# Routing of a part spread over seven half-pairs of units, its column sums beside the router products, and the scatters of the first two parts later

## What is computed

```
x = x + xattn(layernorm(x), ctx_1024, Wq, Wk, Wv, Wp, bp, ln_g, ln_b)
x = x + ffn(layernorm(x), W_gate_router, expert_bias, Wg, Wu, Wd, Wg_s, Wu_s, Wd_s)

# xattn: 16 heads of 16; q and k are layer-normed per head, q scaled by 0.5
attn = softmax(einsum(q, k)); out = (attn @ v) @ Wp.T + bp

# ffn, for each row x of 4096: 8 experts of width 192, the two best are taken
scores = sigmoid(x @ W_gate_router)
_, sel = top_k(scores + expert_bias, 2)
w      = scores[sel] / (scores[sel].sum() + 1e-20)
out    = silu(x @ Wg_s) * (x @ Wu_s) @ Wd_s                    # shared expert
out   += sum over the two of w * (silu(x @ Wg[e]) * (x @ Wu[e])) @ Wd[e]
```

## The kernel before

| unit | 15 | 16 | 17 | 18 | 19 |
|---|---|---|---|---|---|
| part 0 before | scored, best(0) | taken(0), best(1) | taken(1), counted | sums_of, weights | places_of |

## Time and profile before

### The profile page before, as it was taken

The page is one execution under the profiler, slowest core; times in us unless marked ns, Lnnn a source line. Parts: engine busy times, 40 slices in busy tenths (PEclk is TensorE's granted clock), DMA queues, the critical chain, the costliest instruction groups (busy, mean ns, idle before and its releaser), DMA issues.

```text
span 578.1 us, 11042 instructions
## 1 busy us (share of the span) xinstructions
PE 495.2 (86%) x2876; PEld 286.7 (50%) x2877; DVE 344.2 (60%) x1028; ACT 241.4 (42%) x470; POOL 232.4 (40%) x206
## 2 busy tenths in 40 slices
PE   4827879999978988988898993599999999999990
PEld 3724324444434443333554551376676676676660
DVE  5776447767788768645779622155555555555550
ACT  0255767788867776766421110122222222222210
POOL 5354222111111473045114545046646546655534
PEclk9956989999999999989999999699999999999996
DMA  8911911111111221033325574245655656756634
GB/s 274 358 71 27 367 45 43 51 38 38 37 38 37 75 93 56 19 111 128 113 97 175 177 227 173 74 74 83 108 102 83 117 84 93 118 92 86 118 44 46
DMA packets 43766, 60.58 MB, mean 105 GB/s; under 512 B 6512, under 2 KB 34800, under 8 KB 43120
## 3 DMA queue, kind: packets, MB, share of 16 engines
q1 hardware_dynamic: 28688, 36.92, 20.8%
q0 software_dynamic: 15040, 23.21, 20.7%
HBM read 33.77 MB, written 29.52 MB: 109 GB/s over the span
## 4 chain that ended last, share of the span: by engine, by line
PE 52%; DVE 16%; DMA 10%; issue 8%; ACT 8%; POOL 4%; POOLq 1%; SPq 1%; DVEq 0%; ACTq 0%
PE bankS L1050 15%; PE bankS L1066 9%; PE bankV L896 5%; DMA sorted_rows<-XR,route 4%; DMA out<-VR,attn 4%; PE bankR L771 3%; PE bankQ L771 3%; POOL sorted_rows L495 3%; ACT attn L642 3%; PE bankV L900 2%; PE bankS L883 1%; PE bankD L1039 1%; PE bankQ L1057 1%; PE bankV L1039 1%; PE bankR L1057 1%
## 5 line engine op out<-in xcount | busy, mean ns | idle before, releaser
L550 POOL DMA_INDIRECT out<-VR,attn x72 | 111.2, 1544 | 101.0 <-DVE VR L1466 53.4
L1050 PE MATMUL bankS<-experts,scores_in 128*128 x288 | 104.7, 496 | 1.5 <-issue 0.6
L495 POOL DMA_INDIRECT sorted_rows<-XR,route x64 | 63.3, 989 | 96.9 <-DVE XR L1338 23.3
L642 ACT ACTIVATE attn<-bankS,bias 128x512 f32<-128x512 f32 x128 | 81.0, 681 | 11.2 <-PE bankS L871 11.1
L1066 PE MATMUL bankS<-experts,scores_in 96*128 x288 | 74.3, 380 | 1.1 <-DVE scores_in L1457 1.1
L747 ACT ACTIVATE scores_in<-bankS 128x192 f32<-128x192 f32 x72 | 23.8, 330 | 109.6 <-PE bankS L1050 102.4
L1050 PEld LDWEIGHTS bankS<-experts,scores_in 128*128 128x128 f32 x288 | 52.3, 192 | 33.6 <-issue 10.5
L896 PE MATMUL bankV<-attn,VS 128*32 128x512 f32 x256 | 63.5, 619 | 5.3 <-DVE OTT L1245 4.0
L898 PE MATMUL bankD<-attn,ON 128*32 128x512 f32 x256 | 63.5, 619 | 0.0
L1451 DVE TENSOR_TENSOR scores_in<-scores_in,bankS 128x192 f32<-128x192 f32 x72 | 25.5, 354 | 51.4 <-ACT scores_in L747 40.0
L435 POOL DMA_DIRECT2D x_in<-in_xT x13 | 9.5, 734 | 113.7 <-PE bankQ L771 112.7
(11 more groups left out here) (253 smaller groups left out, 864.7 us busy)
## 6 DMA issues: line engine op xcount, KB each, us to landing
VS<-sorted_rows SPq DMA_DIRECT2D x72, 130.0 KB
x_cols<-X2T SPq DMA_DIRECT2D x16, 256.0 KB, 2.2
out<-X SPq DMA_DIRECT2D x8, 512.0 KB
x_in<-in_xT POOLq DMA_DIRECT2D x15, 256.0 KB, 3.2
scores_in<-x_cols SPq DMA_DIRECT2D x14, 256.0 KB
experts<-in_wgu SPq DMA_DIRECT2D x2, 1536.0 KB, 9.5
X<-in_x SPq DMA_DIRECT2D x1, 2048.0 KB, 16.7
experts<-in_wd SPq DMA_DIRECT2D x2, 768.0 KB, 16.8
```

The costliest lines, as they stand in the source:

```text
L495: pool.indirect_dma_start(sorted_rows.rearrange("s p r -> (s p) r"), bass.IndirectOffsetOnAxis(ap=index, axis=0), rows, None, bounds_check ...
L550: pool.indirect_dma_start(out, bass.IndirectOffsetOnAxis(ap=dest[:, i:i + 1], axis=0), y_out[:, i % 4], None, bounds_check=B * N + SPARE - ...
L642: act.activation(Pb[:, u % 2, c, :], bankS[:, c % GH, :], ACT.Exp, bias=bias[:, b, GH * g + c:GH * g + c + 1] if c < GH else biasR[:, b, g ...
L1050: last = pe.matmul(gate_bank(k)[:, 0:2 * F], x_col[:, k, c * P:(c + 1) * P], rhs, start=(c == 0), stop=(c == KC - 1))
```

## The change

In the loop, the routing of parts 0 and 1 is laid out anew; the steps and their order are the same.

| unit | 15 | 16 | 17 | 18 | 19 | 20 | 23 |
|---|---|---|---|---|---|---|---|
| part 0 now | scored | best(0) | taken(0) | best(1) | taken(1), counted | sums_of, weights | places_of |

Part 1 follows eight units later: scored in unit 23 (behind places_of of part 0), up to places_of in unit 31. Part 2 begins with scored in unit 31, and its best(0) moves into the tail. TensorE's `counts` moves from the unit with piece 6 (10) to the unit with piece 7 (11), ahead of the router products in the same bank; its results go to the last 16 columns of bankR, which those products don't touch, and the wait for `r_based` moves on with it. Part 0's scatters wait for `pv_ready` 22 up to 29. Part 1's scatters are not edited, but their places are now ready in unit 31 and no longer in unit 27.

```
-                        pool.wait_ge(pv_ready, UNITS // 2 + 2 + j // 2)
+                        pool.wait_ge(pv_ready, UNITS - 10 + j // 2)
                         scattered(0, j)
...
-                pe.matmul(bank[:, TT * E:TT * E + E], tri, total, start=True, stop=True)
-                pe.matmul(bank[:, TT * E + E:TT * E + 2 * E], ones, total, start=True, stop=True).then_inc(r_sum, 1)
+                pe.matmul(bank[:, TT * D - 2 * E:TT * D - E], tri, total, start=True, stop=True)
+                pe.matmul(bank[:, TT * D - E:TT * D], ones, total, start=True, stop=True).then_inc(r_sum, 1)
...
                 if m % 2 == 1:
+                    if c >= 1 and step == 3:
+                        counts(c - 1, bankR)
                     logits(bankR).then_inc(lg_ready, 1)
                 elif c >= 1 and step == 0:
                     pe.wait_ge(o_done, 2 * c)
                     logit_rows(bankR)
-                elif c >= 1:
-                    counts(c - 1, bankR)
...
                             if m % 2 == 0:
                                 pe.wait_ge(o_done, m // 2)
+                                if c >= 1 and step == 3:
+                                    pe.wait_ge(r_based, c)
                             else:
                                 pe.wait_ge(x2t_sb, m)
                                 if c >= 1 and step == 0:
                                     pe.wait_ge(r_exp, c)
-                                if c >= 1 and step == 2:
-                                    pe.wait_ge(r_based, c)
...
                         if c >= 0 and step == 1:
-                            taken(0)
+                            best(0)
+                        if c >= 0 and step == 2:
                             best(1)
-                        if c >= 0 and step == 2:
+                        if c >= 0 and step == 3:
                             sums_of(c, bankR)
                             weights()
...
                         c, step = divmod(u // 2 - 7, PP)
+                        if c >= 1 and step == 0:
+                            places_of(c - 1)
                         if c >= 0 and step == 0:
                             scored(c)
-                            best(0)
                         if c >= 0 and step == 1:
+                            taken(0)
+                        if c >= 0 and step == 2:
                             taken(1)
                             counted(c)
-                        if c >= 0 and step == 2:
-                            places_of(c)
...
             shared_first(0)
+            best(0)
             taken(0)
```

More of the change, by code:

```diff
@@ L1324, in sums_of @@
                 dve.wait_ge(r_sum, c + 1)
-                link(dve.tensor_tensor(base, carry, bank[:, TT * E:TT * E + E], ALU.add))
-                dve.tensor_tensor(carry, carry, bank[:, TT * E + E:TT * E + 2 * E], ALU.add).then_inc(r_based, 1)
+                link(dve.tensor_tensor(base, carry, bank[:, TT * D - 2 * E:TT * D - E], ALU.add))
+                dve.tensor_tensor(carry, carry, bank[:, TT * D - E:TT * D], ALU.add).then_inc(r_based, 1)
             def places_of(c):
```

## The result

In the measurement that the prediction is held against, the change takes **596.41 us** (median, 595.07 to 596.97) and the kernel before 583.64: ratio 1.024, 95% interval 1.0194 to 1.0287. That is 2.4% longer, clear of no change, though the lower end of the interval lies just under 2%; 581.0 us, no change by a little, was forecast, and the result lies outside the range. The profiled execution took 595.07 us, its span is 593.2 (before 578.1), its mean granted clock 0.933 (before 0.952). The runs further down show that this is one of two results that the same program has.

A forecast was written before the change was run, and what follows sets the result against it. The end was taken to move with the moment part 2 has its places, which follows the attention loop. Terms 2.3 + 1.4 + 0.1 + 0 - 0.4 - 1.0 = 2.4; 583.44 - 2.4 = 581.0 us, range 577.5 to 585.5.

The forecast's parts named there:

- Part 0, forecast gain 2.3: Units 15 to 21: part 0's routing, spread over more units that each hide a piece, loses 3.4 us against 5.8.
- Pair 22-23, 1.4: Units 22-23: GpSimd's bias add no longer runs beside VectorE's L1243 and stretches it; gain 1.4 us, between 0 and 1.8.
- Pair 24-25, 0.1: Units 23 and 24: more routing in one, less in the other, 2.87 us lost against 2.92; gain 0.1 us.
- Pairs 26 to 29, -0.4: Units 26 to 29: part 1's column sums move to unit 28; loss between 0 and 0.7 us, taken as 0.4.
- kept stretch of low clock: Unit 29: TensorE partly at the low clock, worth about 0.8 us if it goes; assumed to stay.
- The tail, -1.0: Unit 31 holds part 1's places and part 2's scores, so TensorE's late output products wait for VectorE; loss 1.0 us.
- Sum, 2.4: Whole kernel: all gains and losses together, a gain of 2.4 us.
- The scatters, "cost nothing": Part 1's sixteen, 1.27 us each, land by 293.3, before part 2 wants to start at 297.9; 4.6 us to spare.
- Part 1's scatters become the bound: Rival, tail: sixteen scatters without a pause slow down and delay part 2's; 586.0 to 591.3 us, chance 0.07.
- paid elsewhere: Rival: the add meets an L1243 in unit 24 and the tail's best is uncovered; gain 0.8, 582.6 us, chance 0.16.
- Doesn't do what it says: Rival, units 21 and 29: output product waits for the sums, the 2.3 falls to about 0; 583.3 us, chance 0.03.

The follow-up runs named there:

- e12_change_fourth: The change itself, unedited, run again in the fourth session beside the kernel before: 582.02 us, ratio 0.9993.
- e14: The change with one landing wait in the middle of part 1's run of sixteen scatters: 580.64 us, ratio 0.9996.
- e3: The kernel before with part 1's sixteen scatters all waiting for the last unit, then going in one run: 580.38 us, ratio 0.9959.
- e13: The kernel before with part 1's sixteen scatters in one run after unit 31, same edit as e3: 581.88 us, ratio 0.9987.
- e16: The kernel before with part 1's sixteen scatters in one run after unit 31, e13 run once more: 580.01 us, ratio 1.0006.
- e9: The change with part 1's scatters in groups of four, a landing wait between groups, third session: 585.41 us, ratio 1.0056.
- e15: The change with places_of in units 21 and 29 and part 1's scatters in groups of four with landing waits: 581.34 us, ratio 1.003.
- e18: e15 run once more (the change, places_of in units 21 and 29, part 1's scatters in groups of four): 580.57 us, ratio 1.0015.
- e11: The change with part 0's scatters at their old gate (units 18 to 25), third session: 594.28 us, ratio 1.0189.
- e6: The kernel before with only the change's later gate of part 0's scatters (pv_ready 22 to 29): 586.3 us, ratio 1.0087.

## Why the prediction was right or wrong

I take the steps one by one, in e12_change_fourth, where nothing is held up, and then in the measurement of record. Windows of e12, pairs 16-17 to 28-29, then from unit 30 to the late output products and from there to the first scatter of part 2:

```profile
154.72:168.54 13.82, 12.79 (x112) 6.01 (x113) 11.73 (x32) 10.50 (x21) 2.02 (x2) 1.00 0.12 39
168.54:181.79 13.25, 12.39 (x97) 5.65 (x98) 11.22 (x32) 10.48 (x21) 2.02 (x2) 1.00 0.11 40
181.79:195.86 14.07, 13.06 (x117) 6.68 (x119) 11.51 (x42) 10.33 (x20) 0.72 (x1) 1.00 0.12 40
195.86:208.68 12.82, 12.50 (x101) 5.98 (x100) 9.02 (x23) 10.54 (x22) 0.00 (x0) 1.00 0.05 20
208.68:224.17 15.49, 12.78 (x112) 6.07 (x114) 12.77 (x40) 10.54 (x20) 8.93 (x9) 1.00 0.22 79
224.17:236.30 12.13, 9.88 (x80) 3.84 (x81) 6.79 (x20) 8.91 (x16) 4.69 (x6) 1.00 0.16 56
236.30:250.93 14.63, 12.80 (x102) 4.90 (x102) 8.80 (x32) 8.22 (x15) 5.22 (x6) 0.88 0.27 91
...
250.93:273.45 22.52, 18.70 (x119) 6.88 (x118) 13.56 (x37) 13.73 (x24) 5.21 (x6) 0.92 0.22 72
273.45:299.10 25.65, 24.30 (x113) 14.32 (x114) 18.13 (x69) 8.23 (x14) 12.58 (x14) 0.93 0.47 159
```

- **Part 0, forecast gain 2.3.** 44.07 us became 41.14: 2.9. The sign and the place were right, the prices too high: over three bare pairs of 12.76 us they still lose 2.86 us, where 4.15 unscaled and 3.4 scaled were worked out. The unscaled gain of 2.8 came nearer by luck, since it took a price too high from a loss too high. Pairs 16-17 and 18-19 are within 0.05 us of the 13.3 to 13.8 that were named; pair 20-21, the longest as forecast, took 14.07 and not 14.8.
- **Pair 22-23, 1.4.** 1.77. L1243 is at 0.69 us there, where it had 1.73, and the pair is back to 12.82, the bare one's 12.76. The rule of the Trainium skill ("SBUF — State Buffer", section "Who interferes with whom") agrees with both, and what it warned of cost nothing: from unit 20 on no L1243 is over 0.74 us. The prediction called the stretched L1243 the only one of sixteen; the first, at 70.09 in the trace of before, took 1.58 us, also beside adds (69.86 to 71.12).
- **Pair 24-25, 0.1.** -0.18; TensorE's wait for XR in unit 24 of the changed kernel is 2.69 us, 2.66 was worked out.
- **Pairs 26 to 29, -0.4.** -0.9 (25.84 to 26.76). The kept stretch of low clock is there in both, at 0.88. It was priced too low: with the levels 1 and 0.5 a mean of 0.88 over 13.89 us is 3.3 us at the low one (the trace has 3.4, from 249.4 to 252.8), worth up to 1.7 us and not 0.8.
- **The tail, -1.0.** Unit 30 to the late products: 20.16 us before (256.23 to 276.39), 22.52 now, -2.4. In e14, the change with a pause off the path, it is 21.12 at full clock, -0.96: the term was right and the clock is the rest. From there to part 2's first scatter before took 23.96 us, now 25.65, a loss of 1.69 for which the sum has no term. TensorE's L771 shows it, in the chain of before and of e12:

```profile
276.39 1.99 PE bankV L771 x8
278.38 1.73 PE bankD L771 x8
...
273.45 2.51 PE bankV L771 x8
275.96 2.90 PE bankD L771 x8
```

  5.41 us for sixteen products that took 3.72 before (276.39 to 280.11).
- **Sum, 2.4.** By the terms above e12 has 2.9 + 1.8 - 0.2 - 0.9 - 2.4 - 1.7 = -0.5 in place of 2.4: to the start of part 2's scatters, counted from unit 14, before needs 300.35 - 143.66 = 156.69 us and e12 157.12. e14, which had no low stretch in its loop, needs 296.37 - 142.31 = 154.06, 2.6 less. So the working found the gain, and left out that the clock takes it back. Mean granted clock over all executions of the fourth session: change 0.939, before 0.948. Within one kernel's executions there, 0.01 of clock goes with 4.5 to 5 us, so the 0.008 are worth about 4 us, an estimate and a correlation. The lower clock goes with the change's routing and not with the run of scatters: before has 0.945 to 0.948 in the three sessions of its kind, before with the run (e3, e13, e16) 0.946 to 0.948, the eight kernels with the moved routing there 0.938 to 0.944.

  Why is open. e12 is at the 1.2 GHz level in unit 29, in unit 31 and beside the late products, before in unit 29 alone. In these loops each fall comes behind waits of TensorE: in the changed kernel of record it had waited 0.42 and 1.51 us ahead of the first (unit 27). The Trainium skill, "TensorE: Matmul & The Clock Gate", section "Part 1: The HAM clock gate (the "warmup" mystery)", says that the clock follows how busy TensorE has lately been. The falls behind waits fit that, but they don't tell which wait will do it: at the same place e12 waited 1.65 us and kept the full clock. I had kept the one low stretch of before and added none. That is the first step that failed, a term that was missing: about -3 us, 1.4 from unit 30 to the late products and 1.7 in them.
- **The scatters, "cost nothing".** This is the step that failed in the measurement of record. Its own numbers held: each scatter 1.28 us (1.27), the last at 292.45, its last recorded landing at 294.74 (5.2 us at most were allowed, 2.3 needed), part 2's first not released by a landing. In e12 the last starts at 288.72, 288.1 was worked out. What failed is the question: I priced the run for the queue that issues it, and for nobody else. It delayed TensorE's semaphores by up to 12.7 us. The window from the late products to part 2's first scatter, in before and in the kernel of record, says what that was worth:

```profile
276.39:300.35 23.96, 22.62 (x113) 13.15 (x114) 17.03 (x65) 9.10 (x15) 0.62 (x2) 1.00 0.31 109
277.18:314.41 37.23, 25.89 (x113) 14.77 (x114) 18.30 (x69) 8.23 (x14) 12.59 (x14) 0.82 0.32 109
```

  That is 13.3 us more than before and 11.6 more than e12 (25.65). Of the 11.6, 8.8 lie ahead of ScalarE's L755 (18.89 us behind the first late product, 10.09 in e12) and 2.8 behind it, where the clock was at 1.2 GHz from 292.4 to 306.0. Another 3.0 us over e12 were lost in pairs 26 to 29, 29.78 against 26.76 us, at a clock of 0.87 and 0.79 against 1.00 and 0.88.
- **The rivals.** "Part 1's scatters become the bound" had the right place, the right sign, and 586 to 591 us, but another mechanism, a queue that falls behind; its tell, a first scatter released by a landing, did not come. None named what came. The rival "paid elsewhere" put 0.6 us on the best in the tail, which the text on the tail had at 1.0.
- **"Doesn't do what it says".** No wait of L771 for the sums; this holds as forecast.

In the fourth session, without lateness, the forecast of 581.0 stands beside 582.02, and "no change" beside 0.9993. That is in part luck: a gain of 2.4 us was summed up, and none came, since losses that had no term ate it up. In the others it is 14 to 15 us off.

**A better version?** None. e3's 0.9959 of the first session became 0.9987 and 1.0006 when it was run again; where nothing is held up, all variants stand within 0.5% of the kernel before by their ratios. Where semaphores are late, the groups of four (e9) are 10 us under the change, 1.7% of it, and still 3.4 us over before. Places earlier with groups (e15, e18) is the variant I would look at next there: 581.34 and 580.57 in the good sessions, not seen in the other kind.

## What to carry to other kernels

When a change makes one engine issue many DMAs without a pause, ask what the others wait for meanwhile, and not only whether the queue is done in time; here a landing wait between groups of four costs some 2 us each, off the path, and in the session where semaphores were late it took 10 us away. When a trace shows a wait that nothing ended, compare the end of the producer's row with the time at which its semaphore was updated. And before a variant is taken for a cure, run the uncured kernel beside it on the same chip at the same time: four of my variants "cured" a standstill where, by all signs, there was none to cure.

## What the runs showed of the hardware that was not expected

- TensorE's semaphore updates can come up to 12.9 us behind the end of the row (e11; 12.7 in the kernel of record), then one every 0.06 us in the order of the products, beside sixteen scatters issued by GpSimd at 1.28 us each. ScalarE's updates flowed meanwhile: in e6 its exponential started at 275.53, took 0.69, and its semaphore came at 276.23, beside products of TensorE that were 2.4 to 4.4 us late.
- The same program has two results, 595 to 596 us in three sessions and 582 us in a fourth, with the kernel before at 580.5 to 583.6 in all. The kind can be read off the number of landings that the trace holds, 497 to 619 or 1,014 to 1,024 of 1,024; a chip of one number showed both.
- With the loop's stalls in units 16 to 23 made shorter, TensorE's mean clock was lower and not higher: 0.939 for 0.948. In e12 more stretches at 1.2 GHz follow from unit 29 on, in the kernel of record from unit 27 on. That one makes the other isn't shown.
